# Sharing the centre-row product of the correction passes, with the swapped copies made by DMAs on the sync queue

## What is computed

```
x = x + _L0_conv_ref(_gn(x), depthwise, pointwise, attention, global_attention)
x = x + _L1_conv_ref(_gn(x), w)

# L0: a depthwise 3x3 convolution, then three 64x64 channel matrices in a row
dw  = conv(x, depthwise_weights, padding 1, one group per channel)
out = softmax(global) @ (pointwise @ (softmax(attention) @ dw))

# L1: signs only
xb  = sign(x)
bw  = sign(clip(w, -1, 1)) * mean(abs(clip(w, -1, 1)))   # mean per output channel
out = conv(xb, bw, padding 1)
```

## Time and profile before

| | |
|---|---|
| three executions | 1843.71, 1844.64, 1845.44 us |
| median | 1844.64 us |
| the profiled execution, first to last instruction | 1841.7 us |
| busy: TensorE matmuls, VectorE, ScalarE, GpSimd | 96%, 87%, 72%, 32% |
| DMA | 271 MB, mean 147 GB/s |

### The profile page before, as it was taken

How to read it: one execution, slowest core, us unless ns; L and a number is a source line. 1 busy time by engine, 2 the same in 40 slices (tenths; PEclk the granted TensorE clock), 3 DMA queues, 4 the chain that set the end, 5 groups by cost and what they waited for, 6 DMA issues and landing times.

```text
span 1841.7 us, 76040 instructions
## 1 busy us (share of the span) xinstructions
PE 1763.1 (96%) x33132; PEld 1571.6 (85%) x33132; DVE 1596.8 (87%) x2581; ACT 1333.7 (72%) x1460; POOL 580.3 (32%) x353
## 2 busy tenths in 40 slices
PE   0499999999999999999999999999999999999997
PEld 0499998998799998999989888898989999899886
DVE  6888899888989889888898888988899888977776
ACT  2377777777677777777777777777767777777774
POOL 1233333333233332333333333333323332333331
PEclk9999999999999999999999999999999999999999
DMA  9735655566556565556656655556655666333324
GB/s 303 181 105 161 159 148 152 161 154 154 145 145 172 153 153 146 155 161 159 153 146 162 157 151 150 143 167 159 150 150 150 163 157 157 96 82 80 77 72 104
DMA packets 278623, 271.37 MB, mean 147 GB/s; under 512 B 16112, under 2 KB 278320, under 8 KB 278464
## 3 DMA queue, kind: packets, MB, share of 16 engines
q1 hardware_dynamic: 269568, 260.11, 54.4%
q10 hardware_dynamic: 8448, 8.39, 1.5%
q0 software_dynamic: 448, 0.73, 0.2%
HBM read 134.95 MB, written 134.22 MB: 146 GB/s over the span
## 4 chain that ended last, share of the span: by engine, by line
PE 95%; SPq 2%; DVE 1%; DMA 1%; issue 0%; ACT 0%; DVEq 0%; ACTq 0%
PE psA L520 82%; PE psB L520 13%; SPq L263 2%; DMA ring<-in_x 1%; DVE ring L964 0%; PE psL L485 0%; DVE psL L960 0%; PE psL L478 0%; DVE bnt L749 0%; DVE ring L969 0%; DVE aggr L865 0%; DVE xh L989 0%; ACT rnd L424 0%; DVE xc L922 0%; DVEq L111 0%
## 5 line engine op out<-in xcount | busy, mean ns | idle before, releaser
L520 PE MATMUL psA<-xh,W 64*64 64x512 f16 x17912 | 1550.9, 373 | 5.8 <-DVE xh L989 5.8
L520 PEld LDWEIGHTS psA<-xh,W 64*64 64x64 f16 x17912 | 1120.4, 106 | 101.1 <-issue 41.3
L520 PE MATMUL psA<-xl,W 64*64 64x512 f16 x9216 | 987.9, 376 | 0.0
L315 POOL TENSOR_TENSOR xl<-xc,xn 128x1024 f16<-128x1024 f32 (+1 forms) x320 | 570.7, 1793 | 1185.6 <-ACT xn L392 1173.6
L520 PEld LDWEIGHTS psA<-xl,W 64*64 64x64 f16 x9216 | 599.3, 107 | 25.5 <-issue 0.6
L520 PE MATMUL psB<-pk,W 64*64 64x512 f16 (+2 forms) x4944 | 608.2, 362 | 2.0 <-DVE pk L941 1.9
L396 ACT ACTIVATE xh<-xc 64x1024 f16<-64x1024 f32 (+2 forms) x622 | 574.4, 941 | 9.2
L392 ACT ACTIVATE xn<-xc 128x1024 f16<-128x1024 f32 (+2 forms) x262 | 270.7, 1036 | 269.3 <-PE psA L520 183.1
L930 DVE SCALAR_TENSOR_TENSOR ring<-psA,columns,ring 128x1024 f32<-128x1024 f32 x256 | 328.3, 1282 | 124.5 <-PE psA L520 124.0
L520 PEld LDWEIGHTS psB<-pk,W 64*64 64x64 f16 x4944 | 305.6, 106 | 61.0 <-issue 35.5
L749 DVE BATCH_NORM_STATS2 bnt<-ring 128x6 f32<-128x512 f32 x512 | 325.8, 681 | 35.0 <-DMA ring<-in_x 34.8
(11 more groups left out here) (101 smaller groups left out, 106.0 us busy)
## 6 DMA issues: line engine op xcount, KB each, us to landing
out_y<-ring SPq DMA_DIRECT2D x512, 256.0 KB, 3.3
ring<-in_x SPq DMA_DIRECT2D x448, 256.0 KB, 4.0
ring<-in_x SPq DMA_DIRECT2D x16, 512.0 KB, 16.8
ring<-in_x ACTq DMA_DIRECT2D x16, 512.0 KB, 15.9
pk<-in_w1T POOLq DMA_DIRECT2D x2, 144.0 KB, 6.2
ring<-in_w1n POOLq DMA_DIRECT2D x2, 144.0 KB, 6.9
grp<-in_same_group POOLq DMA_DIRECT2D x1, 64.0 KB, 7.3
ring<-in_dw POOLq DMA_DIRECT2D x2, 2.2 KB, 6.7
```

The lines of the kernel that those rows point to most:

```text
L315: ins = nc.gpsimd.tensor_tensor(xl[:, slot:slot + rows, 1:W + 1], xc[:, j:j + rows], xn[:, k:k + rows, 1:W + 1], ALU.subtract)
L520: mm = pe.matmul(bank[out0:out0 + C, c0:c1], weights[src0:src0 + C, :], src[src0:src0 + C, slot:slot + rows, width[0]:width[0] + width[1]] ...
```

## The change

**TensorE's products.** For both rows of a pair (an even and the odd row below it) the correction needs the centre-row weights times that row, and other weights times its partner. The kernel after writes this as the centre-row weights times the sum of the two rows, the same for both, and weights less the centre-row weights times the partner. It forms the sums of row pairs (`sh` from the high part, `sl` from the rest), multiplies those once (`shared_rows`, into one bank `psP` that was half of `psL`), copies the result to float16 (`pf`), and adds it to two rows of psA by a product with a scaled identity `idw` (`add_shared`), in slot 3 of the next step. The other correction products use differences of weights (`W0l[:, :, 0]`, `W0h[:, :, 3]`). A step has 30 slots; in each stream one slot of the sum products has only 256 columns (slot 14 of the straight stream, slot 16 of the crossing one):

```
+            def shared_rows(ch, dx, cross, src, wt, first, second, start=False, stop=False):
+                for half, rows in ((0, (0, 3)), (1, (1, 2))):
+                    count = 1 if half == 0 and ch.at(NC - 1) else 2
+                    lo, hi = 0 if first else 1, count if second else 1
+                    if lo < hi:
+                        at, step = rows[lo], rows[1] - rows[0]
+                        k0 = C * (1 - half if cross else half)
+                        mm = pe.matmul(psP[C * half:C * half + C, lo * W:hi * W], wt[k0:k0 + C, :],
+                                       src[k0:k0 + C, at:at + step * (hi - lo - 1) + 1:step, dx:dx + W],
+                                       start=start, stop=stop)
+                return mm
+            def add_shared(n, cross):
+                ch = Chunk(n % NC)
+                at = 2 * n % 4
+                for g, out0 in ((0, C if cross else 0), (1, 0 if cross else C)):
+                    bank, k0 = bank_of(ch, g), C * g
+                    if g == 1:
+                        places = [(at, 2, 0)]
+                    elif ch.at(0):
+                        places = [(at, 1, 1)]
+                    elif at == 0:
+                        places = [(3, 1, 0), (0, 1, 1)]
+                    else:
+                        places = [(at - 1, 2, 0)]
+                    for k, (pos, rows, c) in enumerate(places):
+                        mm = pe.matmul(bank[out0:out0 + C, c * W:(c + rows) * W], idw[k0:k0 + C, :],
+                                       pf[k0:k0 + C, pos * W:(pos + rows) * W], start=False,
+                                       stop=k + 1 == len(places))
+                return mm
...
+            def crossing(t, k):
+                ch = Chunk(t % NC)
+                if k < 3:
+                    own_high(ch, 1, k, True, k == 0)
+                elif k == 3:
+                    if t > 0:
+                        pe.wait_ge(products_done, t)
+                        pe.wait_ge(pf_rdy, t)
+                        add_shared(t - 1, True)
+                elif k < 7:
+                    if k == 4:
+                        pe.wait_ge(xl_rdy, t + 1)
+                    own_low(ch, 1, k - 4)
+                elif k < 10:
+                    mm = beside_low(ch, 1, k - 7)
+                    if k == 9:
+                        mm.then_inc(cross_left, 1)
+                elif k < 16:
+                    if t >= LAG:
+                        crossing_signs(t - LAG, k - 10)
+                elif k < 18:
+                    if k == 16:
+                        pe.wait_ge(sums_straight, t + 1)
+                    shared_rows(ch, k - 15, True, sh, W0l[:, k - 15, 1, :], k == 17, True)
+                elif k < 21:
+                    if k == 18:
+                        pe.wait_ge(sl_rdy, t + 1)
+                    mm = shared_rows(ch, k - 18, True, sl, W0h[:, k - 18, 1, :], True, True, stop=k == 20)
+                    if k == 20:
+                        mm.then_inc(sums_done, 1)
+                else:
+                    if k == 21:
+                        pe.wait_ge(straight_left, t + 1)
+                    if k < 24:
+                        own_high(ch, 0, k - 21, True, False)
+                    elif k < 27:
+                        own_low(ch, 0, k - 24)
+                    else:
+                        beside_low(ch, 0, k - 27)
+                    if k == 29 and ch.at(0):
+                        for dx in range(3):
+                            first_row(ch, dx, True, False)
+                        for dx in range(3):
+                            first_row(ch, dx, True, True)
+            def straight(t, k):
+                ch = Chunk(t % NC)
+                if k < 3:
+                    own_high(ch, 0, k, False, k == 0)
+                elif k == 3:
+                    if t > 0:
+                        add_shared(t - 1, False).then_inc(a_mm, 1)
+                elif k < 7:
+                    beside_high(ch, 0, k - 4)
+                elif k < 10:
+                    own_rest(ch, 0, k - 7)
+                elif k < 13:
+                    mm = beside_rest(ch, 0, k - 10)
+                    if k == 12:
+                        if ch.at(0):
+                            for dx in range(3):
+                                first_row(ch, dx, False, False)
+                            for dx in range(3):
+                                mm = first_row(ch, dx, False, True)
+                        mm.then_inc(straight_left, 1)
+                elif k < 15:
+                    if k == 13:
+                        pe.wait_ge(sh_rdy, t + 1)
+                        if t > 0:
+                            pe.wait_ge(pf_rdy, t)
+                    mm = shared_rows(ch, k - 13, False, sh, W0l[:, k - 13, 1, :], True, k == 13, start=k == 13)
+                    if k == 14:
+                        mm.then_inc(sums_straight, 1)
+                elif k < 21:
+                    if k == 15:
+                        pe.wait_ge(cross_left, t + 1)
+                    if k < 18:
+                        own_high(ch, 1, k - 15, False, False)
+                    else:
+                        beside_high(ch, 1, k - 18)
+                elif k < 24:
+                    if t >= LAG:
+                        straight_signs(t - LAG, k - 21)
+                elif k < 27:
+                    own_rest(ch, 1, k - 24)
+                else:
+                    mm = beside_rest(ch, 1, k - 27)
+                    if k == 29:
+                        mm.then_inc(products_done, 1)
```

**Sync engine.** The swapped high part `xh`, which ScalarE wrote, and the swapped rest `sl` are now copied from SBUF to SBUF by DMAs in SP's program:

```
+            def swap_high(n):
+                ch = Chunk(n % NC)
+
+                sp.wait_ge(xn_rdy, n + 1)
+                if n >= 2:
+
+                    sp.wait_ge(products_done, n - 1)
+                for (i0, i1), (o0, o1) in ((LO, HI), (HI, LO)):
+                    for slot, j, rows in swaps(ch):
+                        k = buf(ch, j)
+                        sp.dma_start(xh[o0:o1, slot:slot + rows, :],
+                                     xn[i0:i1, k:k + rows, :]).then_inc(xh_in[n % 2], 16)
+
+            def swap_low(n):
...
+                sp.wait_ge(xl_rdy, n + 1)
+                if n > 0:
+
+                    sp.wait_ge(sums_done, n)
...
+                for (i0, i1), (o0, o1) in ((LO, HI), (HI, LO)):
+                    sp.dma_start(sl[o0:o1, 0:rows, :], xl[i0:i1, lo:lo + rows, :]).then_inc(sl_in, 16)
...
             for t in range(ALL):
                 if RING <= t + RING - LAG - 2 < ALL:
                     load_chunk(t + RING - LAG - 2)
+                if t + 1 < ALL:
+                    swap_high(t + 1)
+                    swap_low(t + 1)
                 if t > LAG:
                     store_chunk(t - LAG - 1)
```

**VectorE** drops `pack` and `normalise` and gains two float16 additions of 128 by 1032 elements:

```
+                nc.vector.tensor_tensor(sh[:, 0:rows], xn[:, k:k + rows], xh[:, lo:lo + rows],
+                                        ALU.add).then_inc(sh_rdy, 1)
...
+                nc.vector.tensor_tensor(sl[:, 0:rows], xl[:, lo:lo + rows], sl[:, 0:rows],
+                                        ALU.add).then_inc(sl_rdy, 1)
...
             for t in range(ALL):
                 img, a = divmod(t, NC)
+                sums_high(t)
                 if t > 0:
                     add_layer0(*of(t - 1))
+                if a == SCALE_STEP and img + 1 < NB:
+                    stats_of_group(img + 1)
+                sums_low(t)
                 if t > LAG:
                     add_left(*of(t - LAG - 1))
```

496 lines of the change are left out of this document (221 added, 275 removed).

## The result

| | before | after |
|---|---|---|
| median of four executions | 1844.73 us | 2519.36 us |
| lowest and highest | 1843.71, 1845.44 | 2510.90, 2526.47 |
| profiled execution | 1841.7 us | 2512.3 us |
| mean granted clock of TensorE | 0.999 | 0.915 |

The ratio is 1.365, with a 95% interval of 1.362 to 1.369: slower by 36.5%, where the forecast of 2213 us meant 20%. The time lies outside the range of 2010 to 2370 us.

A forecast was written before the change was run, and what follows sets the result against it. SP's in-order round was taken to bound the kernel: 71 us start, 34 for steps 0 to 4, 216 x 8.51 = 1838, 245 for the last 35, 22 tail, 3 profile offset, 2213 us in all; range 2010 to 2370.

The forecast's parts named there:

- The round: SP's in-order issues and landing wait per step: 8.51 us on average, 8.19 for a chunk with two high-swap issues.
- wait for the store's landing: In SP's program, the load waits for the store just ahead to land; part of the 3.99 us from store to load.
- The steps without loads: The last 35 steps, without loads, landing waits or statistics: taken at 7.0 us each, 245 us.
- short form of the round: SP's round written in general as 5.7 us plus 4.5 times the issue time.
- The waits inside do not add to it: In SP's round: TensorE's sums end at 7.1 us, before the low swap is due at 8.5, so waits add nothing.
- rival 5: TensorE's clock: if pauses of 2.2 us sufficed for the 1.2 GHz level, the kernel comes out near 3300 us; chance 0.03.
- The range of GpSimd's normalise: Normalise on GpSimd: taken at 1.6 us, with 2.07 as its upper price; GpSimd's sum 5.1 us a step, 4.3 to 5.6.
- The issue time: SP's cost to issue a swap: 0.645 us, bounds 0.1 to 0.8; 0.1 us in it is 97 us.
- VectorE's sums: Two new additions of 1032 float16 elements on VectorE, taken at 0.8 us each, 1.39 if slow.
- Rival 2: Exclusion of VectorE and GpSimd bounds above SP: 2440 us at 9.4 a step, 2270 at 8.7; chance 0.14.
- Rivals 3 and 4: Swaps issued in about half the time, 2060 us, chance 0.15; contiguous copies costing SP next to nothing, 1714 us, chance 0.06.

The follow-up runs named there:

- e12: e5 with one more edit: ScalarE writes the swapped high part itself, so only the low sum is swapped by DMA; 2012.31 us.
- e9: The changed kernel with eight pairs of unused matmuls ahead of TensorE's wait for `xh`, in steps 3 to 27 of each image; 2473.65 us.
- e2: The changed kernel with normalise moved from GpSimd back to the end of VectorE's step, SP's order kept; 2439.89 us.
- e1: The changed kernel with the two swaps placed ahead of the load in SP's program; 2248.08 us.
- e3: The changed kernel with the edits of e1 and e2 together: swaps ahead of the load, normalise on VectorE; 2192.32 us.
- e5: e3 with VectorE forming the low sum right behind the high one, before GpSimd's low part begins; 2027.00 us.
- e13: e12 with `add_right` moved ahead of the statistics in VectorE's order; 1936.20 us.
- e14: e12 with GpSimd adding only 8 of pack's 130 columns, so it doesn't compute the layer; 1913.35 us.

## Why the prediction was right and wrong

**Right: direction and bound.** Moving two calls in SP's program gave 271 us and taking the high swap away 268; relieving GpSimd gave 79, and that mostly where no loads are. With the high swap gone and the low one between store and load (e12), SP waits for others. The round has the form that was forecast: 8.37 us where no wait falls into it, for 8.19.

**Wrong: the size, 306 us.** Per step with loads, in us:

| term | forecast | measured |
|---|---|---|
| issues of load, two swaps, store | 5.48 | 5.70 |
| wait for the store's landing | 2.70 | 2.87 |
| turns between groups | 0.33 | 0.35 |
| waits inside the round (sums, VectorE, xn) | 0 | 0.72 |
| step | 8.51 | 9.64 |

Forecast terms are those of the prediction, 3.99 split into 1.29 of issue and 2.70 of wait; the turns measured are what is left of 9.64. 216 x 1.13 = 244 us. The steps without loads gave 35 x 1.40 = 49. The rest, 13, is the start (step 5, the first with a load, begins at 114.1 us and not at 105) and a profile that lies 7 us under the median where 3 was added. The prediction's short form of the round, 5.7 + 4.5 x issue time, should have read 5.6; nothing hangs on it.

1. **"The waits inside do not add to it"** is the step that failed, and with it the dismissal of rival 5, the clock. Counted from the end of the high swap's issues, the prediction had TensorE's step begin at 2.4 us and end its sums at 7.1, with the low swap due at 8.5. Measured, the step begins at 3.4: the high swap lands 3.9 us after its issue begins (page, median of those of 129 KB) and not about 3. At the 2.4 GHz level the sums take 4.95 from there and are ready at 8.3, still ahead of the low swap (0.12 us of wait, all of it the turn). In 81 of 198 steps part of the stretch was at the 1.2 GHz level; there the sums take 6.93, end after the low swap is due, and SP stands still. Behind them lie 102 of the 105 us of this wait, 0.52 us a step of the 0.72. A step that ends late leaves a short pause behind it, so the next one is mostly at full clock (75 of 81). Over 216 steps 0.52 are 111 us, an estimate of what the clock cost; e9 gave back 30 of them net in these steps, with its own matmuls in the way. GpSimd's part is 0.15 a step (e2), 32 us, some of it through the same wait. The store's wait for VectorE (0.15) was not taken apart.
2. **The range of GpSimd's normalise** failed. I took the price of one input from VectorE's ratio (1.6) and called two inputs, 2.07, an upper bound, since one input can't cost more than two. It costs 4.02. Nothing in the trace before had this form on GpSimd, and a bound argued from another instruction was none. That is nearly the whole of 7.0 against 8.40 at the end: with normalise off GpSimd it was 7.15. It also makes GpSimd a bound of its own at 8.4 (e1). The Trainium skill would have sent one the same way ("GPSIMD Engine Reference", Engine selection: on GpSimd "1-input is roughly line-rate", where two inputs are about twice as slow as on VectorE). The trace disagrees for this form: 4.02 us, for 0.80 on VectorE.
3. **The issue time**, named as the largest risk, was right: 0.60 us in the median for a swap and 0.64 for a store, against 0.645. In the mean they are 4% dearer.
4. **VectorE's sums** at 0.8: 0.69 alone, 1.09 in the mean of the kernel after, where GpSimd is in the way of some. Rival 2, the exclusion, was real. Removing it from one instruction gave 165 us in e3 (by e5) and from another 76 in e12 (by e13), but in the changed kernel SP's round covered most of it.
5. **Rival 5, the clock**, was given 0.03 and priced as all or nothing: a pause of 2.2 us in each step, and then either no step or every one at half rate. The pauses are 1.9 us in the mean but unequal, and of 17 steps after 2.0 to 2.5 us, 9 were at the lower level in part. Its price of 3300 us was far off; that it could be left out of the sum was wrong.
6. **Rivals 3 and 4**, issues in half the time or for next to nothing, are out: the issues took what was forecast.

**The floor.** 2.5 slots of 32 went, 131 us at most. What stood against it, in us a step: SP's round 8.9 (kernel after, without the waits inside), GpSimd 8.4 (e1), VectorE with the exclusion at the low sum 8.4 (e3), the long issues of the high swap 7.7 (e5), what is left of the exclusion at normalise 7.3 (e13), late loads 7.2 (e14, read from its waits). Every one is above the 6.83 us of the kernel before, and behind them is VectorE's own work, 6.5. The best version that computes the whole, e13, is 5% slower than the kernel before. Whether a layout exists in which all of these fit under 6.83 was not shown either way. A low swap issued by GpSimd, and a deeper ring so that a load needn't wait for the store just issued, were not tried.

## What to carry to other kernels

Before you give a queue more issues in an in-order program, write out its round with the waits for landings in it. Check the slack of the other waits once more with TensorE at its lower clock, if it will pause; and look first whether the new issues can go between an issue and the wait for its landing: that order was worth 271 us here. An operation that moves to an engine which has never run its form has no upper bound in the trace; time it alone before you build on it. When the bound is removed, list the next ones with their levels before expecting a gain: here they stood between 7.2 and 8.9 us a step.
